# Rotary halves exchanged by transfers, and a new order of each unit's work on TensorE, in a decoder of six blocks

## The chip, the cores and the metric

The kernel runs on one core of a Trainium2 chip. Its metric is the device time in microseconds (us) of one execution, median of several runs. Engines named here: TensorE (PE; PEld its weight loads), VectorE (DVE), ScalarE (ACT), GpSimd (POOL), and SyncE (SP; SPq is its queue, which issues transfers).

## The reference, cut to what matters

The input x is [8, 512, 256] in float32. Six blocks follow each other, each added to x and layer-normed:

```python
x = _layernorm(x + _L0_attn_ref(...))    # a0: 16 heads of 16, latent keys, decay table
x = _layernorm(x + _L0_xattn_ref(...))   # attention to 64 context rows
x = _layernorm(x + _L0_ffn_ref(...))     # butterfly feed-forward
x = _layernorm(x + _L1_attn_ref(...))    # a1: 16 heads of 64, rotary, causal
x = _layernorm(x + _L1_xattn_ref(...))   # x1: 8 heads of 64 over own rows and 64 context rows
x = _layernorm(x + _L1_ffn_ref(...))     # mixture of experts, 2 of 8
```

The rotary part of a1, for queries and keys alike, is

```python
def _rotate_half(x):
    d = x.shape[-1] // 2
    return jnp.concatenate([-x[..., d:], x[..., :d]], axis=-1)
q = q * cos + _rotate_half(q) * sin
k = k * cos + _rotate_half(k) * sin
```

where the keys are `x @ w_down @ w_up_k`. Scores get a causal mask, then softmax, then the product with the values.

## The kernel before, in words

One function, `attention`, builds the three attention stages a0, a1 and x1. Each stage runs over 8 batches; a batch has G groups of four heads (4, 4 and 2 in a0, a1 and x1) and each group has four blocks of 128 query rows, so 16, 16 and 8 units. A unit is one block of query rows for four heads. The loop goes over steps, one unit entering per step, and every engine works on several units at once: scores of unit s in step s (`score_head`, L612; VectorE masks them, takes the maximum and writes them to `t`, L993, then the negated maximum `neg`, L1007), exp of unit s-1 on ScalarE (L810), division by the sum for unit s-2 on VectorE and, in a0 and x1, for two heads on GpSimd (L1015, L854), transposes of unit s-3 on TensorE (L668, L671) with ScalarE copying the result out of PSUM to `pT` (L805), and the product with the values for unit s-4 (`times_values`, L674). In a1 a unit has only as many key blocks as the mask needs (one to four).

Beside this, steps carry works, which `tasks` spreads: projections of queries and keys for the next group ("item", L530 on), the latent rows ("lat"), transposes of x ("xT"), values ("v"), and the output projection of the previous batch ("y", L599). A work in a step has a place j from 0 to 4. The list of `segment_jobs` gives every PSUM result one of four A banks in turn; whoever waits for a bank counts along that list. TensorE writes transposes to two T banks in turn, and values to two O banks.

In a step of the kernel before, TensorE goes through j = 0 to 4 and does for each j: scores of head j, transposes of head j, values of key block j, works placed at j. ScalarE does for each j the copy of transposes, the exp, the works. VectorE does for each j the scores, the division, the works.

Scores in a1 and x1 are matmuls over 64 rows (two heads at a time on two halves of the array), value matmuls write 64 columns (32 in a0); projections and transposes use the whole array.

In a1 each item (two query items and two key items a group, i even for queries) is made twice: once with the weights and once with weights whose halves of each head are exchanged (`wqs`, and the second half of `wupk`). VectorE multiplies the first with `cos` into `rsum` and the second with `sin` into `rsin` (L939). GpSimd adds them (L883), ScalarE copies the sum as its high part to `q_hl` or `k_hl` (L751, L753), GpSimd subtracts that for the low part (L887, L890). ScalarE's high parts stand at the end of its step, after exps and O banks (L824 to L827). The sign of the first half is in the table `sin`.

Of the kernel before, what the change touches and what calls it, by code (L numbers as in the profile page):

```python
# [21 lines left out]
P = 128  # L22
B, S, D = 8, 512, 256
SC = 64
# [188 lines left out]
def attention(nc, sh, kind, w):  # L213
# [68 lines left out]
    def work_jobs(work):  # L282
# [8 lines left out]
        if a1:  # L291
            return [((*work, 0), "dve"), ((*work, 1), "rot")]
        if x1:
            return [(work, "ql")]
        return [(work, ("dve", "kl")[work[2]])]

    def segment_jobs(prev, own, nxt):


        jobs = []  # L300
        for s in range(U if own else LN_STEP):
            found = tasks(s, prev, own, nxt)
            for j in range(5):
                if own and j < (5 if x1 else 4):
                    jobs += [(("score", s, j), "dve")]
                jobs += [job for at, work in found if at == j for job in work_jobs(work)]
        return jobs
# [14 lines left out]
    with ExitStack() as ctx:  # L322
# [48 lines left out]
        if a1:  # L371
            wqs = sb("wqs", [P, DT, IN])
            lat = sb("lat", [P, S])
            wdn = sb("wdn", [P, DT, P])
            wupk = sb("wupk", [P, 2, IN])
# [46 lines left out]
        chain = sem("chain")  # L422
        sems = {"full": a_full, "act": a_act, "dve": a_dve, "xt": xt_done, "v": v_done,
# [43 lines left out]
        if a1:  # L467
            loads += [(wq[:], tiled(w["w_q"])), (wqs[:], tiled(w["w_q_swapped"])), (wdn[:], tiled(w["w_down"])),
                      (wupk[:, 0, :], w["w_up_k"]), (wupk[:, 1, :], w["w_up_k_swapped"]),
# [7 lines left out]
        def _(sp):  # L477
# [3 lines left out]
            if x1:  # L481
                sp.dma_start(ctxT[:], tiled(w["ctxT"][0])).then_inc(ctx_in, 16)
            with sp.Fori(1, B) as b:
# [10 lines left out]
        def _(pe):  # L494
# [13 lines left out]
            def project(seg, turn, b, work):  # L508
# [22 lines left out]
                if a1:  # L531
# [5 lines left out]
                    for sw in range(2):  # L537
                        name = (*work, sw)
                        pe.wait_ge(*seg.empty(turn, name))
                        bank = A[seg.bank(name)]  # L540
                        if i % 2 == 0:
                            for t in range(DT):
                                mm = pe.matmul(bank[:], (wq, wqs)[sw][:, t, col], xT[:, t, :],
                                               start=(t == 0), stop=(t == DT - 1))
                        else:
                            mm = pe.matmul(bank[:], wupk[:, sw, col], lat[:], start=True, stop=True)
                        mm.then_inc(a_full, 1)
# [64 lines left out]
            def score_head(seg, turn, b, u, j):  # L612
# [3 lines left out]
                if qt == 0 and j == 0:  # L616
# [83 lines left out]
            def step(seg, turn, b, s, prev, own, nxt):  # L700
# [4 lines left out]
                for j in range(5):  # L705
                    if own and j < (5 if x1 else 4):
# [3 lines left out]
                    if do_v and j == 0:  # L710

                        pe.wait_ge(t_empty, (b * U + u_v + 1) * T_UNIT + 2)
                        g, qt = divmod(u_v % U, QT)
                        if u_v >= 0 and qt == 0 and (not a0 or g == 0):
                            pe.wait_ge(*(seg.emptied(turn, ("v", 0, N_V - 1)) if a0 else (v_done, b * N_V + (g + 1) * N_V // G)))
                        if qt == 0 and not a0:
                            pe.wait_ge(o_empty, b * N_O + (2 * g + 2 - (N_O if u_v < 0 else 0)))
                        elif qt == 0 and g % 2 == 0:
                            pe.wait_ge(o_empty, b * N_O + (g // 2 + 1))
                    if do_v and (j < keys(u_v % U) // P or (x1 and j == 4)):  # L720
                        times_values(b * U + u_v, u_v % U, j)
                    for at, work in found:
                        if at == j:
                            run(seg, turn, b + (work in NEXT and s >= U - QT), work)
# [1552 lines left out]
```

## Time and profile before

| | |
|---|---|
| median of 3 runs | 4617.55 us (4616.95 to 4618.64) |
| profiled execution | 4615.9 us, its span 4614.1 us |
| PE busy | 3915.6 us (85%) |
| DVE busy | 2717.7 us (59%) |
| ACT busy | 2094.8 us (45%) |
| POOL busy | 1178.2 us (26%) |
| mean granted clock of TensorE | 0.932 |

The span goes from the first to the last instruction. Busy shares are means over stages with different limits: a0 runs to about 1030 us, the cross attention and the butterfly to about 1560, a1 to about 2760, x1 to about 3640, and the experts and the end take the rest. Where an engine has stood idle the profile gives the time and what ended it ("<-" and the releaser); "issue" means that nothing in the profile explains it.

### The profile page before, as it was taken

The numbers are of one execution on the slowest core, as the hardware profiler recorded it, in microseconds if no ns is written. First come the engines' busy times: TensorE is split into PE (matmuls) and PEld (weight loads), VectorE is DVE, ScalarE is ACT, GpSimd is POOL, SyncE is SP. The second block draws the span as 40 slices with busy tenths as digits, with TensorE's granted clock in tenths as the row PEclk, the third lists the DMA queues.
The fourth block names the chain that finished last, engine by engine and source line by source line (L and its number), as shares of the span: only waits on it lengthen the run. The fifth ranks groups of instructions, "written<-read, shape, count | busy, mean of one in ns | idle before, by whom it ended". The sixth has DMA issues, their size and how long they took to land. (4 is left out here: it accounts for less than half of the span.)

```text
span 4614.1 us, 81513 instructions
## 1 busy us (share of the span) xinstructions
PE 3915.6 (85%) x25804; PEld 2614.9 (57%) x25805; DVE 2717.7 (59%) x7518; ACT 2094.8 (45%) x4994; POOL 1178.2 (26%) x980
## 2 busy tenths in 40 slices
PE   6999999996869799999999997999999526999980
PEld 3555555565768555555555565666666414666650
DVE  5888888886867466666665654566656421111116
ACT  4777776772342165455545553555555201111110
POOL 2444444443400132232222211122111251000004
PEclk9999999997789899999999998999999758999995
DMA  2000000001020100000000001000000521000003
GB/s 64 6 6 6 6 6 6 1 1 46 14 85 1 59 6 6 1 6 6 6 1 6 1 1 44 7 6 5 5 6 1 172 105 47 30 30 30 30 30 106
DMA packets 80047, 115.62 MB, mean 25 GB/s; under 512 B 14369, under 2 KB 66017, under 8 KB 78945
## 3 DMA queue, kind: packets, MB, share of 16 engines
q1 hardware_dynamic: 73568, 94.56, 6.1%
q0 software_dynamic: 6144, 16.79, 1.2%
q8 instruction: 187, 3.06, 0.3%
q14 instruction: 148, 1.20, 0.1%
HBM read 63.09 MB, written 31.46 MB: 20 GB/s over the span
## 5 line engine op out<-in xcount | busy, mean ns | idle before, releaser
L805 ACT ACTIVATE a_pT<-a_T 128x512 f32<-128x512 f32 (+3 forms) x1024 | 526.0, 514 | 469.8 <-PE a_T L668 460.2
L810 ACT ACTIVATE a_t<-a_t,a_neg 128x512 f32<-128x512 f32 (+3 forms) x1024 | 650.7, 635 | 97.8 <-DVE a_neg L1007 97.4
L668 PE MATMUL a_T<-ident,a_t 128*128 128x128 f32 x3328 | 554.1, 283 | 6.5 <-ACT a_pT L805 6.2
L1015 DVE TENSOR_SCALAR a_t<-a_t,a_inv 128x512 f32<-128x512 f32 (+3 forms) x768 | 528.0, 688 | 9.0
L668 PEld LDWEIGHTS a_T<-ident,a_t 128*128 128x128 f32 x3328 | 396.6, 142 | 171.1 <-issue 68.4
L629 PE MATMUL a_A<-a_kpad,a_qs 128*128 128x512 f32 x1024 | 393.5, 467 | 72.0 <-DVE a_mx L993 50.8
L883 POOL TENSOR_TENSOR a_rsum<-a_rsum,a_rsin 128x512 f32<-128x512 f32 x128 | 162.7, 1271 | 978.0 <-DVE a_rsin L939 976.9
L854 POOL TENSOR_TENSOR a_t<-a_t,a_inv 128x512 f32<-128x512 f32 x256 | 284.2, 1132 | 477.3 <-DVE a_inv L1011 477.3
L993 DVE CUSTOM_DVE_ANT_0 a_t<-a_A,a_decay 128x512 f32<-128x512 f32 x512 | 343.9, 683 | 85.9 <-PE a_A L629 62.2
L993 DVE CUSTOM_DVE_ANT_0 a_t<-a_A,a_table 128x384 f32<-128x384 f32 (+3 forms) x512 | 247.2, 483 | 171.1 <-PE a_A L640 166.9
L854 POOL TENSOR_TENSOR x_t<-x_t,x_inv 128x576 f32<-128x576 f32 x128 | 158.1, 1257 | 725.0 <-DVE x_inv L1011 725.0
L2072 DVE COPY experts_y<-experts_Y 128x256 f32<-128x256 f32 x72 | 30.6, 425 | 514.0 <-PE experts_Y L2010 514.0
L2022 PE MATMUL experts_H<-ex_w,experts_xgT 128*128 x576 | 268.2, 609 | 47.6 <-ACT experts_xgT L2049 47.6
L629 PEld LDWEIGHTS a_A<-a_kpad,a_qs 128*128 128x128 f32 x1024 | 161.7, 193 | 210.1 <-issue 108.7
L805 ACT ACTIVATE x_pT<-x_T 128x512 f32<-128x512 f32 (+1 forms) x320 | 189.3, 592 | 177.8 <-PE x_T L668 135.7
L2010 PE MATMUL experts_Y<-ex_w,experts_hT 128*128 x1152 | 260.5, 379 | 1.0 <-DVE experts_hT L2081 1.0
L2010 PEld LDWEIGHTS experts_Y<-ex_w,experts_hT 128*128 128x128 f32 x1152 | 218.8, 190 | 61.3 <-issue 35.2
L2113 POOL DMA_INDIRECT combine_got<-moe_results,moe_place x64 | 60.9, 951 | 691.5 <-PEq L2091 658.0
L993 DVE CUSTOM_DVE_ANT_0 x_t<-x_A,x_table 128x512 f32<-128x512 f32 x256 | 170.9, 685 | 107.2 <-PE x_A L640 105.1
L689 PE MATMUL a_O<-a_pT,a_v 128*64 128x128 f32 x2560 | 210.9, 286 | 25.0 <-ACT a_oT L822 23.7
L685 PE MATMUL a_O<-a_pT,a_v 128*32 128x128 f32 x4096 | 221.5, 290 | 3.9 <-ACT a_pT L805 3.9
L640 PE MATMUL a_A<-a_khl,a_qhl 64*128 64x128 f32 (+3 forms) x1536 | 188.0, 350 | 38.5 <-issue 15.4
(275 smaller groups left out, 7387.8 us busy)
## 6 DMA issues: line engine op xcount, KB each, us to landing
ex_w<-in_f_w_dram SPq DMA_DIRECT2D x16, 1024.0 KB, 13.6
moe_sent<-route_zeros SPq DMA_DIRECT2D x1, 9216.0 KB, 29.6
experts_xg<-moe_sent SPq DMA_DIRECT2D x72, 128.0 KB, 2.0
moe_results<-experts_y SPq DMA_DIRECT2D x72, 128.0 KB, 1.7
a_xin<-x_all SPq DMA_DIRECT2D x16, 512.0 KB, 2.9
x_xin<-x_all SPq DMA_DIRECT2D x16, 512.0 KB, 2.9
x_all<-in_x_dram SPq DMA_DIRECT2D x1, 4096.0 KB, 14.5
out_dram<-x_all SPq DMA_DIRECT2D x8, 512.0 KB
```

Source lines behind the costliest of these rows:

```text
L629: mm = pe.matmul(A[seg.bank(name)][:, 0:keys(u)], qs[:, gp, q], kpad[:, gp, hl, j, 0:keys(u)], start=(n == 0), stop=(n == 1))
L640: mm = pe.matmul(A[seg.bank(at)][:, 0:keys(u)], q_hl[r, gp, ql, j // 2, q], k_hl[r, gp, kl_, j // 2, 0:keys(u)], start=(n == 0), stop=(n = ...
L668: mm = pe.transpose(bank[:, kt, :], t_of(u, j, kt * P, (kt + 1) * P), sh.ident[:])
L685: mm = pe.matmul(O[hh][32 * j:32 * j + 32, q], v_sb[:, kt, 8 * hh + 2 * j + par, :], p_tile(u, j, kt), start=(par == 0 and qt == 0 and kt ...
L689: mm = pe.matmul(O[pr][64 * half:64 * half + 64, q], v_sb[:, kt, col], p_tile(u, j, kt), start=(kt == 0), stop=last, skip_group_check=True)
L805: nc.scalar.activation(to, of, ACT.Copy).then_inc(t_empty, 1)
L810: nc.scalar.activation(t_of(u_e % U, j, 0, n), t_of(u_e % U, j, 0, n), ACT.Exp, bias=neg[:, slot, j:j + 1], scale=SCALE, accum_out=total[: ...
L854: nc.gpsimd.tensor_tensor(t_of(u_n % U, j, 0, NK), t_of(u_n % U, j, 0, NK), inv[:, u_n % 4, j:j + 1].to_broadcast([P, NK]), ALU.mult).then ...
L993: nc.vector.tensor_tensor_reduce(t_of(s, j, 0, n), A[seg.bank(name)][:, 0:n], table[:, at:at + n], 1.0, LOWEST, ALU.mult if a0 else ALU.ad ...
L1015: nc.vector.tensor_scalar(t_of(u_n % U, j, 0, m), t_of(u_n % U, j, 0, m), inv[:, u_n % 4, j:j + 1], None, ALU.mult).then_inc(normed, 1)
L2010: mm = pe.matmul(Y[parity][:], hT[:, f, :], w2[:, bass.ds(e, 1), f, :].rearrange("p a d -> p (a d)"), start=(f == 0), stop=(f == FT - 1))
L2022: mm = pe.matmul(H[half][:], xgT[:, dt, :], w1[:, bass.ds(e, 1), dt, half * 512:(half + 1) * 512] .rearrange("p a f -> p (a f)"), start=(d ...
```

## The change

It has two parts. In a1 the second projection of each item is gone, with its weights. ScalarE copies the one projection from PSUM to a new buffer `raw` (four of them), SP moves the halves of each head into each other's place with four transfers of 32 partitions from `raw` to `raw_swapped` (two buffers), and GpSimd multiplies that with `sin` before its sum. VectorE still multiplies the PSUM result with `cos`; it waits for the raw copy, so that it is the last reader of the bank.

```diff
-                    for sw in range(2):
-                        name = (*work, sw)
...
+                    pe.wait_ge(*seg.empty(turn, work))
+                    bank = A[seg.bank(work)]
+                    if i % 2 == 0:
+                        for t in range(DT):
+                            mm = pe.matmul(bank[:], wq[:, t, col], xT[:, t, :], start=(t == 0), stop=(t == DT - 1))
+                    else:
+                        mm = pe.matmul(bank[:], wupk[:, col], lat[:], start=True, stop=True)
...
+            def swap_halves(b, n):
+
+                wait_apart(sp, (weights, 16 * len(loads)), (raw_done, b * 4 * G + n + 1), (sin_done, b * 4 * G + n + 3))
+                for k in range(4):
+                    sp.dma_start(raw_swapped[32 * k:32 * k + 32, n % 2, :],
+                                 raw[32 * (k ^ 1):32 * (k ^ 1) + 32, n % 4, :]).then_inc(swapped[n % 2], 16)
...
+            def raw_copy(seg, turn, b, work):
+                _, g, i = work
+                n = 4 * g + i
+                act.wait_ge(*seg.full(turn, work))
+                act.wait_ge(sin_done, b * 4 * G + n + 1)
+                nc.scalar.activation(raw[:, n % 4, :], A[seg.bank(work)][:], ACT.Copy).then_inc(raw_done, 1)
...
-                            pool.wait_ge(rot_done, b * 4 * G + (4 * g + i + 1))
+                            n = 4 * g + i
+                            pool.wait_ge(swapped[n % 2], b * 32 * 4 * G + 64 * (n // 2 + 1))
+                            nc.gpsimd.tensor_tensor(rsin[:], raw_swapped[:, n % 2, :], sin[:],
+                                                    ALU.mult).then_inc(sin_done, 1)
+                            pool.wait_ge(sin_done, b * 4 * G + (n + 5))
+                            pool.wait_ge(rot_done, b * 4 * G + (n + 1))
                             nc.gpsimd.tensor_tensor(rsum[:, i % 2, :], rsum[:, i % 2, :], rsin[:],
                                                     ALU.add).then_inc(rot_sum, 1)
...
-                    for sw in range(2):
...
+                    name = ("item", g, i)
+                    dve.wait_ge(*seg.full(turn, name))
+                    dve.wait_ge(raw_done, b * 4 * G + (4 * g + i + 1))
+                    nc.vector.tensor_tensor(rsum[:, i % 2, :], A[seg.bank(name)][:], cos[:], ALU.mult)\
+                      .then_inc(rot_done, 1)
```

The second part holds for all three stages. TensorE's step is now: for each j the transposes of head j and the works at j (in a0 and x1 without the values works); in x1 the scores against the context; all values of the unit; in a0 and x1 the values works; the scores of the four heads. ScalarE's step: for each j the copy of transposes and the works at j (in a1 the raw copy), then the four exps, then the rest as before, with a1's high parts at the end. VectorE's step: for each j the division and the works, then the scores of the step and `neg`. In x1 the running maximum starts with the context scores instead of ending with them. The A banks are dealt out in the new order.

```diff
                 for j in range(5):
-                    if own and j < (5 if x1 else 4):
-                        score_head(seg, turn, b, s, j)
                     if do_t and j < T_UNIT:
                         transpose_head(b, b * U + u_t, u_t % U, j)
...
                     for at, work in found:
-                        if at == j:
+                        if at == j and not after_values(work):
                             run(seg, turn, b + (work in NEXT and s >= U - QT), work)
+                if own and x1:
+                    score_head(seg, turn, b, s, 4)
+                if do_v:
...
+                    for kt in range(keys(u_v % U) // P):
+                        times_values(b * U + u_v, u_v % U, kt)
+                    if x1:
+                        times_values(b * U + u_v, u_v % U, 4)
+                for _, work in found:
+                    if after_values(work):
+                        run(seg, turn, b + (work in NEXT and s >= U - QT), work)
+                if own:
+                    for j in range(4):
+                        score_head(seg, turn, b, s, j)
...
-                    if do_e and j == 0:
-                        act.wait_ge(negated, b * U + (u_e + 1))
-                    if do_e and j < 4:
-                        slot, n = u_e % 4, (NK if x1 else keys(u_e % U))
+                    for at, work in found:
+                        if at == j:
+                            (raw_copy if a1 and work[0] == "item" else project)(
+                                seg, turn, b + (work in NEXT and s >= U - QT), work)
+                if do_e:
+                    act.wait_ge(negated, b * U + (u_e + 1))
+                    slot, n = u_e % 4, (NK if x1 else keys(u_e % U))
+                    for j in range(4):
```

`after_values` is true for values works in a0 and x1 (`work[0] == "v" and not a1`). At the start of a1, ScalarE makes for each item the raw copy and then its high part. The transfer of the next batch's x to `xin` now follows the fourth swap of a batch.

## Rows read from the trace of the kernel before

**Rows 1.** By stage: start:end, length, busy PE PEld DVE ACT POOL, clock, DMA share, GB/s

```profile
100.00:1000.00 900.00, 837.08 (x6886) 519.57 (x6886) 757.68 (x1782) 644.10 (x1479) 395.25 (x348) 0.97 0.02 5
1600.00:2700.00 1100.00, 1030.12 (x6437) 620.97 (x6438) 691.10 (x2101) 578.46 (x1689) 311.94 (x243) 0.99 0.01 4
2850.00:3600.00 750.00, 739.54 (x5588) 498.04 (x5589) 463.91 (x1515) 437.82 (x983) 149.06 (x121) 1.00 0.02 5
```

**Rows 2.** Timeline of TensorE, one head of a0: start, duration, line, tiles, count

```profile
500.91 0.43 PE L685 MATMUL a_O<-a_pT,a_v 128*32 128x128 f32 x8
501.27 0.73 PE L629 MATMUL a_A<-a_kpad,a_qs 128*128 128x512 f32 x2
501.83 0.60 PE L668 MATMUL a_T<-ident,a_t 128*128 128x128 f32 x4
502.36 0.43 PE L685 MATMUL a_O<-a_pT,a_v 128*32 128x128 f32 x8
```

**Rows 3.** Timeline of TensorE in a1, with two starts of a batch

```profile
2023.22 0.55 PE L640 MATMUL a_A<-a_khl,a_qhl 64*128 64x128 f32 x6 [2.98 <-issue]
...
2025.35 3.10 PE L543 MATMUL a_A<-a_xT,a_wq 128*128 128x512 f32 x4
2028.29 1.88 PE L543 MATMUL a_A<-a_xT,a_wqs 128*128 128x512 f32 x4
2030.10 0.55 PE L640 MATMUL a_A<-a_khl,a_qhl 64*128 64x128 f32 x6
...
2039.76 0.88 PE L668 MATMUL a_T<-ident,a_t 128*128 128x128 f32 x6
2040.47 1.88 PE L546 MATMUL a_A<-a_lat,a_wupk 128*128 128x512 f32 x4
2042.28 0.79 PE L640 MATMUL a_A<-a_khl,a_qhl 64*128 64x384 f32 x6
2043.00 0.65 PE L668 MATMUL a_T<-ident,a_t 128*128 128x128 f32 x4
2043.59 0.66 PE L689 MATMUL a_O<-a_pT,a_v 128*64 128x128 f32 x8
...
2172.62 0.55 PE L640 MATMUL a_A<-a_khl,a_qhl 64*128 64x128 f32 x6 [2.92 <-issue]
```

**Rows 4.** Timelines of ScalarE and GpSimd around two items of a1

```profile
2151.17 0.62 ACT L751 ACTIVATE a_qhl<-a_rsum 128x512 fp32r<-128x512 f32 x1
2154.41 0.63 ACT L753 ACTIVATE a_khl<-a_rsum 128x512 fp32r<-128x512 f32 x1 [2.61 <-POOL a_rsum L883]
...
2153.10 1.27 POOL L883 TENSOR_TENSOR a_rsum<-a_rsum,a_rsin 128x512 f32<-128x512 f32 x1
```

**Rows 5.** Transfers (size, us to landing), and one issue on SP's timeline

```profile
a_xin<-x_all SPq DMA_DIRECT2D x16, 512.0 KB, 2.9
x_ctxT<-in_ctxT_dram SPq DMA_DIRECT2D x8, 64.0 KB, 1.9
...
3897.56 0.35 SPq L1977 DMA_DIRECT2D moe_results<-experts_y  x1
```

**Rows 6.** Engines in 5 us after a gap in a1 (columns of rows 1)

```profile
2025.00:2030.00 5.00, 5.00 (x10) 2.12 (x10) 0.98 (x2) 1.34 (x5) 0.00 (x0) 0.72 0.00 0
```

**Rows 7.** Timeline of TensorE: output projection of one step of a1

```profile
2093.16 3.72 PE L608 MATMUL a_A<-a_wo,a_oT 128*128 128x256 f32 x16
```

**Rows 8.** Timeline of ScalarE, one head of a0

```profile
501.02 0.60 ACT L805 ACTIVATE a_pT<-a_T 128x512 f32<-128x512 f32 x1
501.51 0.72 ACT L810 ACTIVATE a_t<-a_t,a_neg 128x512 f32<-128x512 f32 x1
502.13 0.19 ACT L810 ACTIVATION_READ_ACCUMULATOR a_t<-a_t,a_neg 128x1 f32 x1
```

**Rows 9.** Timeline of TensorE: first scores of two consecutive steps of x1

```profile
3009.51 0.96 PE L640 MATMUL x_A<-x_khl,x_qhl 64*128 64x512 f32 x6
...
3021.47 0.96 PE L640 MATMUL x_A<-x_khl,x_qhl 64*128 64x512 f32 x6
```

More of the change, by code:

```diff
@@ L295, in work_jobs, with after_values @@
         return [(work, ("dve", "kl")[work[2]])]
+    def after_values(work):
+        return work[0] == "v" and not a1
     def segment_jobs(prev, own, nxt):
@@ L303, in segment_jobs @@
             for j in range(5):
-                if own and j < (5 if x1 else 4):
-                    jobs += [(("score", s, j), "dve")]
-                jobs += [job for at, work in found if at == j for job in work_jobs(work)]
+                jobs += [job for at, work in found if at == j and not after_values(work) for job in work_jobs(work)]
+            if own and x1:
+                jobs += [(("score", s, 4), "dve")]
+            jobs += [job for at, work in found if after_values(work) for job in work_jobs(work)]
+            if own:
+                jobs += [(("score", s, j), "dve") for j in range(4)]
         return jobs
@@ L422, in attention @@
         chain = sem("chain")
+        raw_done = env.sem("raw_done") if a1 else None
+        swapped = [env.sem(f"swapped{i}") for i in range(2)] if a1 else None
+        sin_done = env.sem("sin_done") if a1 else None
         sems = {"full": a_full, "act": a_act, "dve": a_dve, "xt": xt_done, "v": v_done,
@@ L536, in project @@
                         pe.wait_ge(a_act, b + 1)
-                    for sw in range(2):
-                        name = (*work, sw)
[L539 to L547, printed above, removed]
+                    pe.wait_ge(*seg.empty(turn, work))
[5 more added lines that the diff above has]
+                        mm = pe.matmul(bank[:], wupk[:, col], lat[:], start=True, stop=True)
+                    mm.then_inc(a_full, 1)
                     return
@@ L615, in score_head @@
                 q = slice(qt * P, (qt + 1) * P)
-                if qt == 0 and j == 0:
+                if qt == 0 and j == (4 if x1 else 0):
                     if a0:
@@ L812, in step @@
                                              accum_out=total[:, slot, j:j + 1]).then_inc(exped, 1)
-                    for at, work in found:
-                        if at == j and not (a1 and work[0] == "item"):
-                            project(seg, turn, b + (work in NEXT and s >= U - QT), work)
                 if do_v:
@@ L830, in begin @@
                 for work in START:
+                    if a1 and work[0] == "item":
+                        raw_copy(start, 0, 0, work)
                     project(start, 0, 0, work)
@@ L1021, in step @@
                             run(seg, turn, b + (work in NEXT and s >= U - QT), work)
+                if own:
+                    dve.wait_ge(t_full, (b * U + s + 1) * T_UNIT)
+                    if x1:
+                        name = ("score", s, 4)
+                        wait_apart(dve, (ready, N_READY), seg.full(turn, name))
+                        for i in range(4):
+                            ins = nc.vector.tensor_tensor_reduce(
+                                t_of(s, i, S, NK), A[seg.bank(name)][:, i * SC:(i + 1) * SC],
+                                table[:, 0:SC], 1.0, LOWEST, ALU.add, ALU.max, mx1[:, slot, i:i + 1])
+                        ins.then_inc(a_dve, 1)
+                        dve.wait_ge(*seg.emptied(turn, name))
+                    for j in range(4):
+                        name = ("score", s, j)
+                        wait_apart(dve, (ready, N_READY), seg.full(turn, name))
+                        nc.vector.tensor_tensor_reduce(
+                            t_of(s, j, 0, n), A[seg.bank(name)][:, 0:n], table[:, at:at + n], 1.0,
+                            mx1[:, slot, j:j + 1] if x1 else LOWEST, ALU.mult if a0 else ALU.add, ALU.max,
+                            mx[:, slot, j:j + 1]).then_inc(a_dve, 1)
+                    dve.wait_ge(*seg.emptied(turn, ("score", s, 3)))
+                    nc.vector.tensor_scalar(neg[:, slot, :], mx[:, slot, :], -SCALE, None,
+                                            ALU.mult).then_inc(negated, 1)
                 if x1 and s == LAG_V - 1 and prev:
```

80 lines of the change are left out of this document (30 added, 50 removed).

## The prediction

> **What bounds the kernel now.** I read the table of engines by stage first [rows 1]. It splits the span into the three attention stages that the change touches: a0 (rows from 100 to 1000 us), a1 (1600 to 2700) and x1 (2850 to 3600). TensorE is busy 837 of 900 us in a0, 1030 of 1100 in a1 and 740 of 750 in x1. So TensorE is the bound in all three, and in x1 nothing else counts. The column beside it warns: in a0 VectorE is busy 758 of 900 us (84%) and ScalarE 644 (72%), so in a0 there is little room before another engine becomes the bound. In a1 the same columns stand at 63% and 53%, GpSimd at 28%.
>
> Next the order of time on TensorE. In a0 one head is a score pair, four transposes, eight value matmuls [rows 2]: starts 0.56, 0.53 and 0.36 us apart, 1.45 us a head, 5.8 us for a step without other work. In a1 six transposes followed by another full-array matmul take 0.71 us, 0.111 each with 0.05 left; four of them followed by value matmuls (half the columns) take 0.59, so 0.14 us above 4 x 0.111 is the price of changing the array's tiling [rows 3]. The eight value matmuls of a0 fit the same: 0.36 is 2 x 0.111 + 0.14. A batch of a1 (16 steps) lasts 2172.62 - 2023.22 = 149.4 us.
>
> Last, ScalarE and GpSimd around one step with rotary items [rows 4]: ScalarE's two high-part copies (L751, L753) start 3.24 us apart, and before the second it stands still for 2.61 us until GpSimd has done the low part and the sum (1.27). ScalarE runs in order, so the next step's evictions of transposes wait behind this. Today that is free: it is over before TensorE needs a bank.
>
> **The change, part by part.**
>
> *Fewer projections.* Per query item four matmuls go, 1.81 us from start to start; per key item two of the four that take 1.81, so 0.90 [rows 3]. 64 of each: 116 + 58 = 174 us of TensorE time. This would be the gain if TensorE stayed the bound of a1.
>
> *Fewer tiling changes.* Before there are 8 a step in a0, 10 in a1, some 12 in x1; after 2, 3 and 5. At 0.14 that is 0.86, 1.0 and 1.0 us a step. Over 128, 128 and 64 steps: 110, 125 and 67 us if TensorE stays the bound.
>
> *The new chain in a1.* Items come two a step, in two of four steps. Before, VectorE made both products from PSUM. Now: projection, ScalarE raw copy, four transfers on SP, GpSimd's product with sin, GpSimd's sum, ScalarE's high part, GpSimd's low part. ScalarE's high parts still stand at the end of its step, in order, so all this lies between the raw copy and the next step's first eviction. Terms:
> - Swap: an issue on SP takes 0.35 us, about 0.4 with its gap; 64 KB lands after 1.9 us, 512 KB between on-chip buffers after 2.9 [rows 5]. Last of four issued 1.2 after the first, plus 1.9 and 0.1 of semaphore: 3.2 us. No row shows a 64 KB transfer from SBUF to SBUF. Ends: 1.9 (issues hidden) and 4.4 (2.9 + 3 x 0.5). I take 3.2, nearest to the row of equal size.
> - Raw end to first high part: 3.2 + 1.27 (sin) + 1.27 (sum) = 5.8. To the second: the old 3.24 and one more GpSimd operation, 4.5. ScalarE is free 0.5 later: 10.8 us after the first raw copy ends. GpSimd's 1.27 is in [rows 4]; its product with sin, which no row has, reads and writes the same shape.
> - Step with items 0, 1: transposes 0.4, projection 1.8, copy 0.6 and 0.2 of latency: raw copy ends at 3.0, ScalarE is free at 13.8. TensorE has finished the step by about 5 and can run only two transposes and a projection ahead, since the two T banks wait for ScalarE.
> - Step with items 2, 3: projection is ready, raw copy ends 1.3 after the first eviction; 1.3 + 10.8 = 12.1.
> - The two steps without items run at TensorE's pace: eviction and transposes 1.55 and 1.05, v projection 0.95 each, values 1.5 and 1.9, scores 1.3 and 1.5: 10.8. TensorE comes out of a stand of about 9 us. The trace shows what that costs: after 2.98 us of standing still a projection of 4 takes 2.94 us where the next takes 1.81, [rows 3]; over these 5 us the mean granted clock is 0.72, a part at 1.2 GHz and the rest at 2.4 [rows 6]. With the groups beside it about 1.5 us. Together 12.3.
> - A group without y: 13.8 + 12.1 + 12.3 = 38.2. The group with y: its output matmuls (3.5 us a step, [rows 7]) count in the first and fourth step and hide in the stands of the other two: 45.2. The last group: a first step with xT and lat of about 9.3 on ScalarE, raw copy at 10.7, free at 21.5 and 33.6, a last step of 6.3 with 1.5 of slow clock, 41.4, then the loop's gap of 2.9 and its slow start of 1.4: 45.7.
> - Batch: 2 x 38.2 + 45.2 + 45.7 = 167.3, against 149.4: +18 us. Seven such batches +125, the last without next items about +10. At the start of the stage the four items run strictly one after another, about 7.2 us each, where the first scores now come about 14 us sooner; fewer weights to load give 2 back: +12. Sum for a1: +147 us. The 174 and 125 us saved on TensorE are already inside it: they become standing time.
>
> A page of the Trainium skill speaks against the four transfers. "DMA: Bandwidth & Descriptors", section "Rules for kernel authors", says that transfers to disjoint groups of partitions serialize, since each already spreads over all engines. Read strictly the swap would be 4 x 1.9 = 7.6 us; no run here shows it.
>
> *a0.* TensorE's step falls from 5.8 to 4.95. ScalarE's cycle does not: copy and exp are 0.49 and 0.62 apart, and the exp's accumulator read adds 0.1 [rows 8], 1.21 a head, 4.85 a step. In the new order the third eviction must wait for a transpose that waits for the first: about 0.5 us of hole. So 5.4 where 5.8 stood: -0.4 a step, 51 us over 128 steps. The step in which VectorE also makes the padded keys is held by VectorE (84% busy), so I take -40. Ends: -110 (no hole) and 0 (VectorE or ScalarE holds all).
>
> *x1.* The step from 3009.51 to 3021.47 is 11.96 us [rows 9]. New: -1.05 each, 67 in 64 steps. Against it: three of five transposes in a row wait for evictions where no projection stands between, 0.45 in the third and 0.9 in the fourth step of a group; and ScalarE takes up the exps only after the v evictions of the fourth step, now behind the values, so they run 2.5 us into the next step: 0.5. That is 1.85 a group, 30 in 16 groups. I take -37; ends -67 and +10.
>
> Loads, the deleted inputs and the moved xin transfer cost nothing: xin is waited for ten steps later.
>
> **Sum.** The profiled execution has 4615.9 us (span 4614.1), 1.65 under the median of 4617.55. 4615.9 + 147 - 40 - 37 = 4686; on the scale of the median 4687 us.
>
> **Rivals.**
> - *A: TensorE stays the bound everywhere.* 4616 - 174 - 110 - 125 - 67 = 4140. For it: [rows 1]. Against: ScalarE's high parts stand in order behind the chain, and even with a swap of 0 us a batch would only come to about 167.3 - 8 x 3.2 = 142. Chance 0.04.
> - *B: the chain holds a1, but is shorter.* Swap 1.9 takes 1.3 x 8 = 10 off a batch, a clock that stays up another 5: a1 about +30; a0 -55 and x1 -50 because the order is softer than I think. About 4540 to 4605, middle 4575. For it: all overlaps that I left out point there. Against: four issues are in the code. Chance 0.22. The point where the sign turns: a1 batches under 159 us.
> - *C: evictions bound a0 and x1 too.* Two T banks against one copy at a time: a0 and x1 give nothing or lose 10, a1 +150 to +170. 4760 to 4800. For it: ScalarE's 72% in a0. Against: a cycle of 5.4 is still under 5.8. Chance 0.13.
> - *D: the four transfers serialize.* Swap 7.6 instead of 3.2, twice in a group, 31 groups: +270, 4960. Against: they are small beside the 512 KB that land in 2.9. Chance 0.03.
>
> **How the numbers follow.** Forecast, 4640 to 4740: 0.55. A measurement of this kernel tells 0.2% (9 us) from no change; 0.03 for within that, between B and the forecast. Faster: A, B = 0.26. Slower: forecast, C, D = 0.71. The range from 4560 to 4790 leaves out A, D, the low end of B and the high end of C, about 2 in 10. Its own range for the likeliest case: 4640 to 4740.
>
> **What would show it.** In a1: a batch near 167 us; TensorE busy share down to about 75% with its granted clock clearly under 0.98; stands of TensorE of 6 to 9 us, released by ScalarE's a_pT copies, two in each group; ScalarE waiting about 2 us ahead of L751's copy and about 4 ahead of L753's, each on GpSimd's sum; landing of a swap near 1.9 us from its own issue. In a0 a plain step near 5.4 us, in x1 the step with two items near 10.9. The forecast is wrong if ScalarE has no long wait on GpSimd in a1, if the batch there is under 159 us, or if TensorE still shows over 90% in a1.

## The result, and the profile after

The changed kernel takes 4810.6 us (median of four runs, 4803.9 to 4817.5) against 4617.6 of the kernel before: 1.042 times as long, interval 1.040 to 1.044. It is slower, as forecast, but by 193 us where the sum said 69, and it lies 20 us above the range.

Stages are told apart by the first load of each on SyncE's timeline (start, duration, queue, line, tiles). In the kernel after:

```profile
1022.34 0.49 SPq L1194 DMA_DIRECT2D x_xin<-x_all  x1
...
1529.51 0.51 SPq L489 DMA_DIRECT2D a_xin<-x_all  x1
...
2986.02 0.54 SPq L489 DMA_DIRECT2D x_xin<-x_all  x1
```

The same loads start in the kernel before at 1055.36, 1561.78 and 2786.23. So a0 with the setup gained 33 us (forecast 40), the blocks between are the same (507.2 against 506.4), a1 went from 1224.5 to 1456.5, **+232 us (forecast +147)**, and x1 from 846.4 to 841.5 (the expert blocks after it are unchanged), **-5 us (forecast -37)**. The excess over the forecast is 85 in a1 and 32 in x1, with 7 in a0: that is the whole miss of 124 us. Inside a1, six batches in the middle grew by 157 us (forecast 6 x 17.9 = 107); the start with the first batch and the end with the last batch grew by 75 (forecast 40).

The stages by engine, which answers to [rows 1], the third row 200 us later because x1 starts later (start:end, length, busy PE, PEld, DVE, ACT, POOL with counts, granted clock, DMA share, GB/s):

```profile
100.00:1000.00 900.00, 788.24 (x7164) 559.36 (x7166) 825.42 (x1838) 655.24 (x1535) 403.27 (x356) 0.97 0.02 5
1600.00:2700.00 1100.00, 757.40 (x5088) 529.05 (x5089) 521.36 (x1659) 551.27 (x1529) 391.69 (x308) 0.84 0.11 29
3050.00:3800.00 750.00, 689.00 (x5637) 528.66 (x5638) 490.79 (x1520) 436.90 (x993) 151.83 (x124) 0.97 0.02 6
```

In a1 TensorE fell from 94% busy to 69%, and its mean granted clock from 0.99 to 0.84. No engine is near full there, which points to a chain across engines, and the waits name its links (engine, waiting instruction, releaser: us in total, times, longest):

```profile
PE a_T L693 <- ACT a_pT L845: 345.6, 120, 8.1
ACT a_khl L786 <- POOL a_rsum L932: 260.9, 64, 6.7
ACT a_qhl L784 <- POOL a_rsum L932: 177.7, 64, 7.1
PE a_A L665 <- DVE a_rsum L985: 63.7, 31, 8.2
```

One turn of that chain on ScalarE, SyncE and GpSimd, which answers to [rows 4] (start, duration, engine, line, [idle before, releaser]; the rows of SyncE begin at each new issue and merge what follows):

```profile
2104.41 0.60 ACT L807 ACTIVATE a_raw<-a_A 128x512 f32<-128x512 f32 x1 [2.76 <-PE a_A L569]
2105.07 1.16 SPq L498 DMA_DIRECT2D a_rawswapped<-a_raw  x2
2105.63 1.23 SPq L498 DMA_DIRECT2D a_rawswapped<-a_raw  x2
2106.27 1.22 SPq L498 DMA_DIRECT2D a_rawswapped<-a_raw  x2
2108.95 1.27 POOL L928 TENSOR_TENSOR a_rsin<-a_rawswapped,a_sin 128x512 f32<-128x512 f32 x1 [16.80 <-DMA a_rawswapped<-a_raw]
2110.30 1.32 POOL L932 TENSOR_TENSOR a_rsum<-a_rsum,a_rsin 128x512 f32<-128x512 f32 x1
2111.65 0.63 ACT L784 ACTIVATE a_qhl<-a_rsum 128x512 fp32r<-128x512 f32 x1 [2.24 <-POOL a_rsum L932]
2116.21 0.63 ACT L786 ACTIVATE a_khl<-a_rsum 128x512 fp32r<-128x512 f32 x1 [3.93 <-POOL a_rsum L932]
```

The raw copy ends at 2105.01 and the product with sin starts at 2108.95: a swap of 3.94 us, forecast 3.2. The starts of the issues are 0.56 and 0.64 apart, and the fourth, by the last row (two issues over 1.22 us, the last of 0.59), comes at 2106.9, 1.83 after the first; each transfer lands 2.0 us after its own issue. This turn is a typical one: of the 64 pairs of items in a1, the swap of the first takes 3.92 to 4.08 us in 54 and up to 5.1 in the others, mean 4.06. To the first high part it is 6.6 us (forecast 5.8), from there to the second 4.6 (4.5). TensorE meanwhile, answering to [rows 3]:

```profile
2108.57 1.88 PE L569 MATMUL a_A<-a_xT,a_wq 128*128 128x512 f32 x4
2117.37 1.51 PE L693 MATMUL a_T<-ident,a_t 128*128 128x128 f32 x6 [6.91 <-ACT a_pT L845]
2118.67 1.92 PE L571 MATMUL a_A<-a_lat,a_wupk 128*128 128x512 f32 x2
...
2130.64 0.66 PE L693 MATMUL a_T<-ident,a_t 128*128 128x128 f32 x2 [6.46 <-ACT a_pT L845]
```

It stands 6.9 and 6.5 us in the two steps with items, and comes back at half speed (granted clock 0.50 from 2117.3 to 2120.5): six transposes take 1.3 us from start to start where [rows 3] has 0.71, two projections 1.85 where four take 1.81.

### The profile page after: what moved, and what is told of

It is laid out like the page before. It is cut to its first block and busy times, and to the rows that moved or that the text cites. A ratio compares the mean times of both kernels' runs of the same rounds, so it can differ in the third digit from the quotient of the medians.

```text
span 4807.7 us, 81821 instructions
## 1 busy us (share of the span) xinstructions
PE 3645.2 (76%) x25420; PEld 2680.5 (56%) x25421; DVE 2715.0 (56%) x7390; ACT 2154.2 (45%) x5122; POOL 1337.6 (28%) x1108
## 5 line engine op out<-in xcount | busy, mean ns | idle before, releaser
L693 PE MATMUL a_T<-ident,a_t 128*128 128x128 f32 x3328 | 534.2, 301 | 413.0 <-ACT a_pT L845 345.6
L845 ACT ACTIVATE a_pT<-a_T 128x512 f32<-128x512 f32 (+3 forms) x1024 | 485.8, 514 | 224.4 <-PE a_T L693 216.3
L1038 DVE TENSOR_SCALAR a_t<-a_t,a_inv 128x512 f32<-128x512 f32 (+3 forms) x768 | 546.4, 752 | 9.0
L928 POOL TENSOR_TENSOR a_rsin<-a_rawswapped,a_sin 128x512 f32<-128x512 f32 x128 | 163.3, 1276 | 1069.1 <-DMA a_rawswapped<-a_raw 1069.1
L1061 DVE CUSTOM_DVE_ANT_0 a_t<-a_A,a_table 128x384 f32<-128x384 f32 (+3 forms) x512 | 224.1, 487 | 406.1 <-PE a_A L665 405.3
L1061 DVE CUSTOM_DVE_ANT_0 a_t<-a_A,a_decay 128x512 f32<-128x512 f32 x512 | 322.2, 683 | 41.2 <-PE a_A L654 39.4
L654 PE MATMUL a_A<-a_kpad,a_qs 128*128 128x512 f32 x1024 | 288.2, 418 | 34.1 <-DVE a_kl L975 17.6
L1061 DVE CUSTOM_DVE_ANT_0 x_t<-x_A,x_table,x_mx 128x512 f32<-128x512 f32 x256 | 177.1, 748 | 175.1 <-PE x_A L665 173.6
L985 DVE TENSOR_TENSOR a_rsum<-a_A,a_cos 128x512 f32<-128x512 f32 x128 | 88.3, 690 | 277.5 <-ACT a_raw L807 180.8
L665 PE MATMUL a_A<-a_khl,a_qhl 64*128 64x128 f32 (+3 forms) x1536 | 169.8, 345 | 70.3 <-DVE a_rsum L985 63.7
L714 PEld LDWEIGHTS a_O<-a_pT,a_v 128*64 128x64 f32 x2560 | 152.7, 149 | 94.1 <-issue 63.2
```

The source lines that it names most:

```text
L654: mm = pe.matmul(A[seg.bank(name)][:, 0:keys(u)], qs[:, gp, q], kpad[:, gp, hl, j, 0:keys(u)], start=(n == 0), stop=(n == 1))
L665: mm = pe.matmul(A[seg.bank(at)][:, 0:keys(u)], q_hl[r, gp, ql, j // 2, q], k_hl[r, gp, kl_, j // 2, 0:keys(u)], start=(n == 0), stop=(n = ...
L693: mm = pe.transpose(bank[:, kt, :], t_of(u, j, kt * P, (kt + 1) * P), sh.ident[:])
L714: mm = pe.matmul(O[pr][64 * half:64 * half + 64, q], v_sb[:, kt, col], p_tile(u, j, kt), start=(kt == 0), stop=last, skip_group_check=True)
L845: nc.scalar.activation(to, of, ACT.Copy).then_inc(t_empty, 1)
L928: nc.gpsimd.tensor_tensor(rsin[:], raw_swapped[:, n % 2, :], sin[:], ALU.mult).then_inc(sin_done, 1)
```

## The experiments

Stage a1 is measured from its first load to that of x1, a turn of x1 by the mean distance of its last five loads of xin. Most edits are made to the changed kernel; code is shown abridged, with "..." where lines are left out. Ratios are to the kernel before, timed on the same chip in the same rounds (some of these chips ran the kernel before in 4598 us), with their 95% intervals.

| kernel | a1, us | turn of x1, us | ratio |
|---|---|---|---|
| before | 1224.5 | 102.1 | 1 |
| after | 1456.5 | 102.4 | 1.042 (1.040 to 1.044) |
| order alone | 1194.2 | 99.1 | 0.981 (0.979 to 0.982) |
| exchange alone | 1512.7 | 103.2 | 1.064 (1.062 to 1.066) |
| high parts deferred | 1095.1 | 102.4 | 0.964 (0.962 to 0.966) |
| one transfer | 1377.9 | 102.3 | 1.024 (1.023 to 1.026) |
| no transfer | 1268.8 | 102.3 | 1.002 (1.001 to 1.003) |
| values behind scores | 1456.5 | 96.9 | 1.035 (1.033 to 1.036) |
| deferred + values | 1094.5 | 97.0 | 0.956 (0.955 to 0.958) |
| the same, two projections | 1151.7 | 96.3 | 0.969 (0.967 to 0.970) |
| after, layer norm later | 1459.8 | 102.3 | 1.042 (1.040 to 1.044) |
| deferred + values + layer norm | 1084.9 | 97.1 | 0.956 (0.954 to 0.958) |
| after, 128 waits | 1457.1 | 98.8 | 1.039 (1.037 to 1.040) |
| after, 64 waits | 1456.4 | 105.5 | 1.045 (1.043 to 1.046) |

**Order alone.** The kernel before with the new order on all engines; both projections stay. The lines are cut against the changed kernel.

```
-  return [(work, "rot")]
+  return [((*work, 0), "dve"), ((*work, 1), "rot")]
...
-  (raw_copy if a1 and work[0] == "item" else project)(...)
+  if at == j and not (a1 and work[0] == "item"): project(...)
```

> The new order of the steps alone, with the second projection of every item kept in the causal stage, so no exchange through transfers. Theory one (the loss is ScalarE's two in-order copies of the high parts, which wait for the exchange): the causal stage, 1224 us before and 1456 after, stays within 30 us of 1224, the other two stages keep their after lengths (1022 and 841), and the time is 4560 to 4610. Rival (the order itself starves TensorE in the causal stage, whoever computes the exchanged half): the causal stage keeps over half of the 232 us, over 1340, and the time is over 4690.

4529.95 us. Theory one holds, though the time is 30 us below its range: the order by itself shortens a1 by 30 us and the whole by 88. Those 30 are far from the 125 us of a1 that the forecast's rival A put on fewer tiling changes. x1 did not keep its length as expected: it takes 824.9 us here against 841.5 in the changed kernel, because the same code makes a turn in 99.1 us here and in 102.4 there.

**Exchange alone.** Raw copies, transfers and GpSimd's product in the old order of steps (cut against the kernel before).

```
+  sp.dma_start(raw_swapped[32*k:32*k+32, n % 2, :], raw[32*(k^1):32*(k^1)+32, n % 4, :])
...
   if own and j < 4: score_head(...)     # as before, inside the loop over heads
```

> The exchange through transfers alone, with the order of the steps as before in all three stages. Theory one: the causal stage is 1400 to 1470 us long and the time 4790 to 4870, with waits of ScalarE for GpSimd's sums of about 4 to 7 us twice in a group of four steps and TensorE released by ScalarE's copies of the transposes. Rival (the order is what costs): the causal stage loses the 16 second projections of a batch and is 1170 to 1260, the time 4560 to 4650.

4910.8 us, 1.064 times the kernel before. The mechanism of theory one holds, its size does not: a1 is 288 us longer than before, 43 beyond the stated end, and the time 41 us beyond it. The exchange carries all of the loss, and the new order gives back 56 of it. ScalarE's waits for GpSimd's sums are 269.2 us (L773) and 261.8 (L775) in 64 pairs, so 4.2 and 4.1 each: in this order both high parts wait long.

**High parts deferred.** ScalarE's two high parts go from the end of their own step to the end of the next, the sums get four buffers, GpSimd's low parts follow.

```
-  rsum = sb("rsum", [P, 2, S])
+  rsum = sb("rsum", [P, 4, S])
...
-  for _, work in found:
-      if a1 and work[0] == "item": project(...)
+  for _, work in tasks(s - 1, prev, own, nxt):      # a1 only
+      if work[0] == "item": project(...)
```

> The changed kernel with ScalarE's high parts of each pair of items moved from the end of their own step to the end of the next step, four buffers of sums instead of two, and GpSimd's low parts moved behind them. The exchange, its 64 transfers a batch and GpSimd's products are the same. Theory one: the exchange is hidden, TensorE's 346 us of standing for ScalarE's copies of transposes falls below 80 us, a batch of the causal stage goes from 177 to about 140 (before's 149.4 less 40 matmuls of 0.22 us), and the time is 4480 to 4560, below that of the kernel before. Rival (the chain through the transfers limits the stage by its own throughput, on GpSimd, SyncE or the layer norm's share of VectorE): the stage stays over 1380 us and the time over 4730.

4454.15 us: 356 below the changed kernel with the same 512 transfers and the same products, 164 below the kernel before, and 26 below the range expected. TensorE's standing for ScalarE's copies falls from 345.6 to 60.1 us. The rival, that the chain limits by its throughput, is out. Place, buffers and low parts move together here, so the run does not tell how much each is worth. The two high parts no longer wait, from its timeline of ScalarE:

```profile
2099.47 0.60 ACT L807 ACTIVATE a_raw<-a_A 128x512 f32<-128x512 f32 x1 [3.00 <-PE a_A L569]
2101.45 0.60 ACT L807 ACTIVATE a_raw<-a_A 128x512 f32<-128x512 f32 x1 [0.45 <-PE a_A L571]
2103.48 0.62 ACT L784 ACTIVATE a_qhl<-a_rsum 128x512 fp32r<-128x512 f32 x1
2104.00 0.62 ACT L786 ACTIVATE a_khl<-a_rsum 128x512 fp32r<-128x512 f32 x1
```

They start 0.52 us apart, where they stood 4.56 apart above. ScalarE now waits for TensorE, and a1 is busy again (columns as above, 1000 us of it), though a batch, 129.0 us by its loads of xin (mean of five), is not the 140 of the expectation but shorter:

```profile
1600.00:2600.00 1000.00, 862.70 (x6427) 612.81 (x6427) 773.27 (x2101) 678.82 (x1924) 472.99 (x372) 0.94 0.15 37
```

The expectation had a wrong price: it took off 40 matmuls of 0.22 us. By [rows 3] four take 1.81 us, so 0.45 each, and the counts of the two traces (768 projection matmuls in eight batches before, 384 after) make 48 a batch: 21.7 us, and 149.4 - 21.7 = 127.7.

**One transfer.** One transfer of 128 partitions in place of four of 32. It leaves out the exchange: the halves stay where they are.

```
-  for k in range(4):
-      sp.dma_start(raw_swapped[32 * k:32 * k + 32, n % 2, :], ...)
+  sp.dma_start(raw_swapped[:, n % 2, :], raw[:, n % 4, :]).then_inc(swapped[n % 2], 16)
```

> The changed kernel with the exchange as one transfer of 128 partitions instead of four of 32; the halves are not exchanged, so the rotary result is left wrong. It prices the three further issues on SyncE, 0.6 to 0.7 us each in the trace after against the 0.4 that the forecast took. Theory one (the stage is as long as the chain from ScalarE's raw copy to its high part, eight times a batch): 1.9 us less in each of the 8 pairs of a batch, 15 us of 177, some 120 us in all, so 4670 to 4710, and raw copy's end to GpSimd's product falls from 3.9 to about 2.1 us. Rival (the issues are beside other work): within 30 us of 4811.

4714.25 us, ratio 1.024 against 1.042, 4 us above the range expected. Stage a1 is 79 us shorter, not 120: three issues fall away, but the single transfer lands later. Its tile on SyncE (duration min/median/max in ns, then us to landing), the changed kernel's after it:

```profile
L497 SPq DMA_DIRECT2D a_rawswapped<-a_raw x128: 464/465/749, 1555.1 to 2828.7; - x128
...
DMA to landing us min/median/max: 2.2/2.3/3.7
```

```profile
L498 SPq DMA_DIRECT2D a_rawswapped<-a_raw x512: 507/590/1753, 1553.8 to 2907.4; - x171
...
DMA to landing us min/median/max: 1.9/2.0/3.4
```

And the same link of the chain as above, in a batch of the kernel with one transfer:

```profile
2233.25 0.60 ACT L805 ACTIVATE a_raw<-a_A 128x512 f32<-128x512 f32 x1 [1.42 <-PE a_A L567]
...
2236.27 1.28 POOL L926 TENSOR_TENSOR a_rsin<-a_rawswapped,a_sin 128x512 f32<-128x512 f32 x1 [14.08 <-DMA a_rawswapped<-a_raw]
...
2238.92 0.63 ACT L782 ACTIVATE a_qhl<-a_rsum 128x512 fp32r<-128x512 f32 x1 [0.97 <-POOL a_rsum L930]
```

Raw copy's end to product is 2.42 us and to the high part 5.07. In 54 of the 64 pairs the first is 2.36 to 2.44; the other ten reach up to 3.85, and the mean is 2.55. So the swap is 1.51 us shorter on average than with four transfers, 97 us over the 64 pairs, and a1 follows with 79: 0.81 us for each us of swap. Its batch takes 166.5 us (mean of five) and the changed kernel's 175.7. The forecast's own sum, with 2.55 put in for its 3.2, would give 162.1, so its other terms are some 4 us a batch too small here.

**No transfer.** GpSimd multiplies the raw copy itself. This too leaves out the exchange of the halves.

```
-  pool.wait_ge(swapped[n % 2], ...)
-  nc.gpsimd.tensor_tensor(rsin[:], raw_swapped[:, n % 2, :], sin[:], ALU.mult)
+  pool.wait_ge(raw_done, b * 4 * G + n + 1)
+  nc.gpsimd.tensor_tensor(rsin[:], raw[:, n % 4, :], sin[:], ALU.mult)
```

> The changed kernel without the transfers: GpSimd multiplies ScalarE's raw copy itself, so the halves are not exchanged; all copies, products, sums and their order stay. It prices the whole way through the transfers. Theory one: 3.8 us less per pair than the changed kernel, 30 us of a batch's 177, 240 in all, so 4560 to 4600; ScalarE's wait for GpSimd's sums in both parts of a pair stays near 2.5 and 4 us, since GpSimd's three products per item remain. Rival (the chain's length is not what the stage follows, the four cold clocks and the layer norm are): over 4680.

4606.5 us, 1.002 of the kernel before. The way through the transfers is worth 188 us of a1's 232; 240 were expected, and the time is above the range of 4560 to 4600. Of ScalarE's waits only the second part's stayed (252.7 us in 64); the first's fell to 21.8, under the 2.5 a pair that I expected. The other 44 us are there with no transfer at all, although TensorE does 16 projections a batch less. TensorE now stands 123.7 us for a bank that VectorE's cosine product holds and 109.7 for ScalarE's copies. That three GpSimd operations per item in line with ScalarE's order cost more than VectorE's product did is the likely reason; no run separates it.

**Values behind scores.** In x1 alone the value projections, 5 us of matmuls, stand between the scores and the loop's jump, and their evictions behind the exponentials.

```
-  for _, work in found: (values) run(...)
   if own: for j in range(4): score_head(...)
+  for work in late: run(...)                # x1 only
```

> The changed kernel with one order undone in the last attention stage alone: the value projections stand behind the scores on TensorE (and their evictions behind the exponentials on ScalarE), so that some 5 us of matmuls stand ahead of the loop's jump instead of 1.7. Theory two (the stage gained only 5 us of 37 because TensorE now stands about 3 us at the jump of each turn and restarts at the low clock): the gap with the release 'issue' at the turn goes, the stage goes from 841 to 805 to 820 us and the time to 4775 to 4790. Rival (the jump costs the same wherever it stands): the stage stays within 8 us of 841 and the time within 10 us of 4811.

4778.2 us; a turn falls from 102.4 to 96.9. The number is as expected, the theory behind it only in part, as the order alone had hinted and the next two show.

**128 and 64 satisfied waits** ahead of everything in TensorE's program of x1.

```
+  for _ in range(128 if x1 else 0):         # 64 in the second
+      pe.wait_ge(pv, 2)
   pe.wait_ge(weights, 16 * len(loads))
```

> The changed kernel with 128 satisfied waits put ahead of all else in TensorE's program of the last attention stage, where it stands 20 us anyway; they only move where the code behind them lies. The kernel with the order alone has the same code in this stage without the stand of 3 us at each turn of the loop. If the stand depends on where the loop's code lies, it changes by over 1 us a turn, 8 to 25 us in all (99 us a turn where it goes, from 102.4). If it depends on how little work stands ahead of the jump, a turn stays 102.4 and the time within 10 us of the changed kernel.

> The same with 64 satisfied waits. By place: a stand at the turn that differs from the one with 128, or from the 3.0 us with none. By queued work: the same 3.0 us in all three.

4776.4 and 4805.3 us (ratios 1.039 and 1.045; the changed kernel has 1.042). The place where a turn ends, on TensorE's timeline, first in the changed kernel, then with 64 waits:

```profile
3189.22 1.66 PE L665 MATMUL x_A<-x_khl,x_qhl 64*128 64x512 f32 x12
3193.91 1.97 PE L693 MATMUL x_T<-ident,x_t 128*128 128x128 f32 x8 [3.03 <-issue]
3195.66 2.57 PE L589 MATMUL x_A<-x_xT,x_wq 128*128 128x512 f32 x4
```

```profile
3191.76 1.65 PE L667 MATMUL x_A<-x_khl,x_qhl 64*128 64x512 f32 x12
3199.33 1.86 PE L695 MATMUL x_T<-ident,x_t 128*128 128x128 f32 x8 [5.92 <-issue]
```

With 128 waits there is no such stand at all, and a turn takes 98.8 us, as in the order alone (99.1). Over the turns the stand is 2.6 to 3.0, 5.2 to 6.0 or 0 us with the same instructions behind 0, 64 or 128 others. So it depends on where the loop's code lies, not on the work. "issue" says only that nothing in the profile's engines explains the stand, but the record of transfers shows more. In one turn of x1 its row of instruction packets (queue, packets, MB, share) is in the changed kernel and with 64 waits alike

```profile
q8 instruction: 9, 0.15, 0.6%
```

and there is no such row in a turn of the kernel before, of the order alone, of the 128 waits or of the two projections below: exactly the kernels without a stand. The packets are of 16 KB. In the changed kernel one starts within 0.4 us of the beginning of each stand looked at. With 64 waits there are two in each, 3.0 to 3.8 us apart, and the stand is about twice as long. So in these kernels the loop fetches its code anew in every turn, and TensorE stands where a fetch is not there in time. That the packets are TensorE's code is inferred from their timing. A turn of a1 has ten such packets before and after alike. The Trainium skill's page "Runtime: NRT & Kernel Launch", section "Instruction fetch mechanics", says that a branch to code outside the blocks held on the engine waits for a fetch. The trace agrees: nine packets a turn with a stand, none without.

Queued work covers only a part of the stand: with the values behind the scores 0.3 to 0.9 us were left of it, and without any stand (the kernel with two projections, 96.3) a turn is a further 0.6 to 0.7 shorter.

**Both edits**, deferred high parts and values behind scores.

```
   the two diffs above, in one kernel
```

> The deferred high parts in the causal stage and the value projections behind the scores in the last stage, in one kernel. The two stages do not touch each other: 4454 less the 32 us that the second edit gave alone, 4415 to 4430. If the second edit's gain depends on where the program's code comes to lie, as the last stage's 99.1 us a turn in the kernel with the order alone against 102.4 here suggests, the sum fails by 10 us or more.

4399.75 us, ratio 0.956: 4.4% faster than the kernel before. The product of the single ratios is 0.964 x 1.035 / 1.042 = 0.957, so the edits add. The microseconds fell below the expected 4415 since this chip runs the kernel before 20 us faster.

**The same with two projections** on TensorE in place of the exchange.

```
-  raw copy, transfers, nc.gpsimd product with sin
+  for sw in range(2): matmul(bank, (wq, wqs)[sw]...); VectorE multiplies by (cos, sin)[sw]
```

> The same as the kernel with both edits, but with the exchanged halves computed by second projections on TensorE, as in the kernel before, instead of by the raw copy, the transfers and GpSimd's product. It asks whether the exchange is worth anything once nothing waits for it. Theory one: TensorE bounds the causal stage in both, so 40 matmuls of 0.22 us more per batch, 8.8 us of about 129, 70 us in all: 4480 to 4500. Rival (the transfers and the raw copies cost as much as they spare): within 20 us of the kernel with both edits.

4455.0 us, 0.969, below the expected 4480 to 4500. Once nothing waits for it, the exchange is worth 57 us of a1 (theory: 70); in the place where the change had put it, it costs 262 (1456.5 against 1194.2). That the theory came near is luck. Its 8.8 us a batch rests on the wrong price named above; by [rows 3] TensorE is spared 21.7, and a batch is only 9.7 shorter (129.0 against 138.7). TensorE is 86% busy with the exchange and 93% without it, so it no longer bounds the stage alone.

This kernel also shows what the deferral is worth without any exchange. In a1 it differs from the order alone by the deferral with its buffers only, and takes 1151.7 us against 1194.2. So 42 of the 361 us that the deferral gave the changed kernel have nothing to do with the transfers.

**Layer norm later**, on the changed kernel and on the one with both edits.

```
-  if own and prev and LN_STEP <= s <= LN_STEP + 1: advance(norm[0], 2)
+  if own and prev and LN_LATE <= s <= LN_LATE + 1: advance(norm[0], 2)   # two steps later in a1
```

> The changed kernel with the causal stage's layer norm of the batch before given to VectorE two steps later, in the two steps of a group that hold no items. It prices the extra stand in the third group, where the second pair of scores waits 5.8 us for a bank that VectorE's cosine product holds, behind six small layer-norm operations of which some take 1.22 us while GpSimd works and 0.16 otherwise. If that stand is a term of its own: 5 to 6 us less in each of seven batches, 30 to 45 us, 4755 to 4785. Rival (TensorE only stands later for ScalarE's high parts, which the exchange sets anyway): within 12 us of the changed kernel.

> The same edit on top of the kernel with deferred high parts and the values behind the scores. There a stand of 6.9 us a batch in that place is the longest left (2161.53 in its trace, released by VectorE's cosine product). If it goes, 7 batches by 5 to 6 us: 35 to 45 us less, 0.95 of the kernel before, a batch near 124 us. If VectorE, busy 100 of a batch's 130 us, is what bounds that group, the stand only moves and under 12 us go.

Both misses, the rivals hold. On the changed kernel TensorE's standing for VectorE's cosine product fell from 63.7 to 32.5 us, and that for ScalarE's copies rose from 345.6 to 372.8: the stand moved one link on, and a1 is 3 us longer. On the better kernel a1 lost 10 us where I expected 35 to 45, and the ratios of the two cannot be told apart.

## Why the prediction was right and wrong

- *Direction and mechanism: right.* TensorE was not to stay the bound of a1; ScalarE's in-order high parts behind the exchange were. The signs named came: 6.9 and 6.5 us stands released by a_pT copies, waits on GpSimd's sum of 2.2 and 3.9 us, busy share and clock down; only the batch, 175.7 us, was not near 167. The deferral shows it by experiment: one change of place, with two more buffers, gives 361 us back. Even TensorE's fall went beyond the forecast "about 75%", to 69%.
- *The step that failed: the term "Swap", "an issue on SP takes 0.35 us, about 0.4 with its gap".* It came from a row of another transfer [rows 5], though the trace of before had a nearer one: its issues of `xin`, between on-chip buffers, take 0.49. This issue takes 0.59 (median), and the fourth starts 1.83 us after the first instead of 1.2; the landing of 2.0 was right. So a swap is 3.94 us in the turn shown and 4.06 on average, in place of 3.2. Counted as the forecast counts, 0.86 us in 64 pairs, that is 55 of the 85 us missed in a1; at the 0.81 that the single transfer gave it is 45. Both are estimates from these rows. Both ends had been named (1.9 to 4.4), but the range of the sum took in the lower one alone.
- *The other 30 to 40 us of a1* are open. About 6 lie at the start of the stage, where the first scores come 18 us later and not 12. The forecast's sum had no term for VectorE's cosine product, for which TensorE stands 63.7 us, but halving that stand by moving the layer norm changed nothing. The sum also errs more as the swap gets shorter: by 1.5 us a batch with four transfers (174.2 with 4.06 put in, 175.7 measured), by 4 with one and by some 10 with none. So it was nearest where the chain was longest.
- *x1, -37 forecast, -5 measured.* Two terms failed. The order's own effect was rated too high: where there is no stand at the jump, x1 is 21.5 us (order alone) to 25.3 us (128 waits) shorter than before. A two-item step did fit: 10.5 us (3163.92 to 3174.39), forecast 10.9. The -1.05 us a step in the sum is also 0.98 by its own price of 0.14, which is some 4 us in all. The other 17 to 20 of the 32 us are the loop's jump, for which the sum held no term. In a1 the trace of before shows that stand [rows 3]; in x1 it shows none, and I took this for a property of the stage. It takes back 3.3 to 3.6 us a turn.
- *The range.* It was left only because both missed: without the 32 us of x1, or without the 45 to 55 of the swap, the time would have been inside 4560 to 4790.
- *a0, -40 forecast, -33 measured: right.* A plain step went from 5.8 to 5.47 us (507.90 to 513.37), forecast 5.4.
- *Rival A* (TensorE stays the bound, 4140 us) is out, and not for the place of the high parts alone: with them deferred the kernel takes 4454 us and TensorE is 86% busy in a1. *Rival D* (the four transfers serialize, 7.6 us) is out: each landed 2.0 us after its own issue, 0.6 apart. The Trainium skill's "DMA: Bandwidth & Descriptors", § "Rules for kernel authors", says that transfers to disjoint halves of the partitions serialize; the trace disagrees only with the reading that whole latencies add up. In the turn shown the packets of each transfer moved in about 0.44 us, and those of the next began after them, so whether two could move their bytes side by side is not shown. *Rival C* was wrong in its reason, since a0 did gain, though its 4760 to 4800 came nearest to the time.
- *"Even with a swap of 0 us a batch would only come to about 142"*: without transfers a batch in the middle of the stage takes 152.3 us (mean of five). The chain without the transfers is longer than the sum says.

## What to carry to other kernels

Before moving work off the busiest engine, look at what waits in program order behind the last link of the new chain: here two copies at the end of a step turned a saving of 57 us into a loss of 262, and one step's delay with two more buffers turned it back. The same delay was worth 42 us even without the new chain. A term that stands on a loop's critical chain must be priced from both sides in the sum and in the range, because its error is multiplied by the turns of the loop. When two kernels with the same code in a stage differ there by a constant per turn, look at the loop's jump on each engine, and count the instruction packets of a turn, before explaining it by the work.

## What the runs showed of the hardware that I had not expected

A quarter of the partitions is not a quarter of the price: issuing a transfer of 32 partitions took 0.59 us and landing 2.0, of 128 partitions 0.465 and 2.3. The latencies of four in a row overlap, and their issues are what adds up.

A loop's jump on TensorE costs between 0 and 6.0 us of standing by the place of its code, and within a run it comes back turn after turn (105.3 to 105.8 us a turn with 64 waits). It goes with the instruction fetches of the loop, nine packets of 16 KB a turn or none, and the profile's record of transfers shows them.

GpSimd holds VectorE up even on tiny tiles. In the kernel with both edits, layer-norm operations on 128x4 elements take 0.16 us alone and 1.22 beside a GpSimd product:

```profile
2156.80 0.16 DVE L170 SCALAR_TENSOR_TENSOR a_scratch<-a_scratch 128x4 f32<-128x4 f32 x1
...
2158.26 1.26 POOL L939 TENSOR_TENSOR a_rsum<-a_rsum,a_rsin 128x512 f32<-128x512 f32 x1
2158.32 1.22 DVE L173 SCALAR_TENSOR_TENSOR a_scratch<-a_scratch 128x4 f32<-128x4 f32 x1
2159.60 1.26 POOL L935 TENSOR_TENSOR a_rsin<-a_rawswapped,a_sin 128x512 f32<-128x512 f32 x1
2159.64 1.23 DVE L167 TENSOR_TENSOR a_scratch<-a_scratch 128x4 f32<-128x4 f32 x1
```

VectorE's two long ones end at 2159.54 and 2160.87, GpSimd's at 2159.52 and 2160.86: they look like waits for GpSimd's end, not like slow work. All 72 operations of these three lines in a1 agree: the 25 that began while GpSimd was at work ended within 0.03 us after it, and the 47 others took 0.15 to 0.17 us.
